# First attention of a two-layer block on one core: heads in pairs, scores computed twice

## The chip, the core and the metric

The kernel runs on one core of a Trainium2 chip. The metric is the time of one execution on the device, in microseconds. PE is the matrix engine, PEld its weight loads, DVE the vector engine, ACT the scalar engine, POOL GpSimd, and SP the engine that issues most DMAs. Each engine runs its own instruction stream in order; they meet at semaphores (`then_inc`, `wait_ge`).

## The reference

The input x is 4 x 512 rows of 256. Everything is computed in float32:

```
_L0_attn_ref:                     # 16 heads of 16, causal, B = 4, S = 512
q, k, v = heads(x @ Wq.T), heads(x @ Wk.T), heads(x @ Wv.T)
sim = where(causal, (q @ k.T) * 16 ** -0.5, -inf)
out = merge(softmax(sim) @ v) @ Wo.T

x = x + layernorm(_L0_attn_ref(layernorm(x), Wq, Wk, Wv, Wo))
x = x + layernorm(_L0_ffn_ref(layernorm(x), ...))
```

`_L0_ffn_ref` is a second causal attention (16 heads of 128), a shared gated layer and 16 routed experts of which each row takes four.

## The kernel before

Rows are in tiles of 128, four tiles to a batch. After the projections (phase 1, to the first `meet`) q and k lie transposed and split in a high and a low fp32r part, `q1_hl` (in the memory of `xT`) and `k1_hl`; v lies in `v1` (the memory of `hs`), all for 8 groups of 8 heads (128 rows are 8 heads of 16). A score in nearly full precision needs hi x hi + lo x hi + hi x lo. So a head's operands are stacked in 64 rows of `stk`: three copies of 16 rows, and one matmul sums the three products.

In the first attention 64 heads follow each other, a step (`step1`) each, written out except for a loop over two periods (`run_steps`). The engines work as a pipeline, with the values one step behind the scores:

- PE, every second head: `stack` selects the operands of a pair with a 0/1 matrix `sel` (L1462), into the banks 5 and 6; ACT copies them to `stk` (L769).
- PE: `scores`, four matmuls for the query tiles of 512, 384, 256 and 128 keys (L1545), banks 0 to 2.
- DVE: `mask_and_max` adds the causal mask in PSUM and gives the negated maximum of each query (L1092). ACT: the exponential into `p1`, with the sum (L816). DVE: reciprocal and multiplication (L1162, L1168).
- PE: `turn`, ten 128 x 128 transposes of the probabilities (L1555); DVE and ACT copy them to `pT1` (L1146, L825).
- PE: `values_of`, four fp32 matmuls against `v1_pad`, the head's 16 columns of v in 128 otherwise zero columns (L1567), so that 8 heads add up in bank 7 (`O1_BANK`). POOL fills `v1_pad` (`fill_v`, L455) up to six heads ahead. After 8 heads DVE copies bank 7 to `oT1`.

Between batches the finished batch is projected (`project_y`), normalised, added to x (`make_x1`) and normalised twice more for the second layer, spread over the steps of the next batch: PE and ACT for the copies, POOL for a chain of small operations on four numbers a row (`norm_y` and `norm_x1`, with `rsqrt` by three Newton steps, each operation waiting for the one before in `link`), ACT and DVE for the scaling (`scale_u`, `scale_xn`). What is left of the last batch runs beside the second attention. POOL also splits the weights of the second attention's first pair, before its first `fill_v` of the loop.

SP loads the inputs, issues one DMA that blanks 34 MB of `xs_rows` in HBM for the expert stage (L373), and then waits for the end of the first attention.

## Time and profile before

| | us |
|---|---|
| median of 3 runs (1417.71 to 1421.4) | 1419.59 |
| the profiled execution | 1434.26 |
| its span, first to last instruction | 1432.5 |
| PE busy in the span | 1306.9 (91%) |
| DVE busy | 1022.8 (71%) |
| ACT busy | 894.2 (62%) |
| POOL busy | 528.8 (37%) |

The granted clock of PE was 0.968 of full speed over the span. Busy time is the time in which at least one instruction of the engine was in work; matmuls overlap in the records, and an fp32 matmul has two records. In rows, a time in us comes first, then a duration; brackets at the end say how long the engine had been idle and who ended that.

### The profile page before, as it was taken

The numbers are of one execution on the slowest core, as the hardware profiler recorded it, in microseconds if no ns is written. First come the engines' busy times: TensorE is split into PE (matmuls) and PEld (weight loads), VectorE is DVE, ScalarE is ACT, GpSimd is POOL, SyncE is SP. The second block draws the span as 40 slices with busy tenths as digits, with TensorE's granted clock in tenths as the row PEclk, the third lists the DMA queues.
The fourth block names the chain that finished last, engine by engine and source line by source line (L and its number), as shares of the span: only waits on it lengthen the run. The fifth ranks groups of instructions, "written<-read, shape, count | busy, mean of one in ns | idle before, by whom it ended". The sixth has DMA issues, their size and how long they took to land.

```text
span 1432.5 us, 27089 instructions
## 1 busy us (share of the span) xinstructions
PE 1306.9 (91%) x7836; PEld 1125.4 (79%) x7836; DVE 1022.8 (71%) x3118; ACT 894.2 (62%) x2433; POOL 528.8 (37%) x868
## 2 busy tenths in 40 slices
PE   5999989989989989999999999999998878999940
PEld 4766766667669979999999899998997757999930
DVE  6588888978956757677877678667876655555536
ACT  3577766767757668776786767876676542444422
POOL 1300230412333344354364424734335251444434
PEclk9999999999999999999999999999999998999975
DMA  9993000000011331101122111211021333333353
GB/s 333 335 335 103 2 1 2 1 0 1 1 32 51 99 105 60 60 31 60 49 86 74 53 38 60 86 64 60 30 72 48 109 101 98 117 119 120 116 200 134
DMA packets 83615, 123.38 MB, mean 86 GB/s; under 512 B 7476, under 2 KB 68148, under 8 KB 83220
## 3 DMA queue, kind: packets, MB, share of 16 engines
q1 hardware_dynamic: 76612, 102.83, 22.5%
q0 software_dynamic: 6864, 18.88, 3.6%
q8 instruction: 65, 1.06, 0.3%
q14 instruction: 74, 0.61, 0.1%
HBM read 66.50 MB, written 55.18 MB: 85 GB/s over the span
## 4 chain that ended last, share of the span: by engine, by line
PE 71%; DVE 12%; issue 5%; ACT 4%; POOL 3%; DMA 2%; SPq 2%; another core or an unknown queue 1%; POOLq 0%; DVEq 0%; ACTq 0%
PE bank L1462 45%; PE bank L1567 8%; PE bank L1823 5%; PE bank L1641 4%; PE bank L1555 3%; DVE bank L1092 3%; PE bank L1545 3%; PE bank L1802 1%; PE bank L1833 1%; DVE hs L1313 1%; ACT p L928 1%; DMA yl<-ys_rows 1%; SPq L383 1%; DVE pT L1300 1%
## 5 line engine op out<-in xcount | busy, mean ns | idle before, releaser
L1092 DVE CUSTOM_DVE_ANT_0 bank<-bank,mask 128x512 f32<-128x512 f32 (+3 forms) x512 | 238.8, 518 | 36.3 <-PE bank L1545 18.3
L919 ACT ACTIVATE p<-bank,stat 128x512 f32<-128x512 f32 (+3 forms) x256 | 131.5, 526 | 133.3 <-DVE stat L1092 133.2
L1567 PE MATMUL bank<-pT,v_pad 128*128 128x128 f32 (+3 forms) x512 | 181.6, 457 | 17.3 <-DVE pT L1146 17.2
L1462 PE MATMUL bank<-xT,w_hl 128*128 128x512 f32 x768 | 190.2, 397 | 3.5 <-DVE hs L1313 3.0
L1462 PEld LDWEIGHTS bank<-xT,w_hl 128*128 128x128 f32 x768 | 145.4, 190 | 38.0 <-issue 3.5
L466 POOL CAST w_hl<-raw_qkv 128x512 fp32r<-128x512 f32 x96 | 58.9, 614 | 312.2 <-DMA raw_qkv<-in_qkvo 163.2
L816 ACT ACTIVATE p<-bank,stat 128x512 f32<-128x512 f32 (+3 forms) x256 | 133.0, 530 | 57.9 <-DVE stat L1092 57.9
L1462 PE MATMUL bank<-pT,v 128*128 128x128 f32 (+3 forms) x768 | 137.0, 327 | 0.0
L1462 PE MATMUL bank<-qk 128*128 128x512 f32 (+3 forms) x768 | 131.1, 320 | 3.0 <-DVE pT L1300 2.6
L928 ACT ACTIVATE p<-p,stat 128x512 f32<-128x512 f32 (+3 forms) x256 | 123.1, 552 | 15.2 <-DVE stat L1316 14.7
L1462 PEld LDWEIGHTS bank<-qk 128*128 128x128 f32 x768 | 120.6, 191 | 12.1 <-DVE v L1294 2.8
L468 POOL TENSOR_TENSOR w_hl<-raw_qkv,w_hl 128x512 fp32r<-128x512 f32 x96 | 124.0, 1292 | 7.8
L1567 PEld LDWEIGHTS bank<-pT,v_pad 128*128 128x128 f32 x512 | 86.1, 193 | 49.9 <-DVE pT L1146 24.8
L1338 DVE TENSOR_TENSOR o<-bank,o 128x512 fp32r<-128x512 f32 x64 | 44.2, 690 | 111.1 <-ACT o L935 91.3
L705 POOL DMA_INDIRECT ys_rows<-mid,goal x79 | 76.5, 968 | 126.5 <-DVE mid L1419 123.9
L1555 PEld LDWEIGHTS bank<-ident,p 128*128 128x128 f32 x640 | 81.3, 143 | 44.2 <-DVE p L1168 19.2
L1462 PEld LDWEIGHTS bank<-pT,v 128*128 128x128 f32 x768 | 109.7, 190 | 2.9
L1462 PE MATMUL bank<-wo_hl,o 128*128 128x256 f32 x768 | 106.9, 288 | 3.3 <-DVE o L1338 1.4
L1462 PEld LDWEIGHTS bank<-w_hl,xT 128*128 128x128 f32 x768 | 99.8, 189 | 12.2 <-issue 4.4
L1300 DVE TENSOR_TENSOR pT<-bank,pT 128x128 fp32r<-128x128 f32 (+3 forms) x256 | 107.5, 482 | 1.4 <-issue 1.0
L1462 PE MATMUL bank<-w_hl,xT 128*128 128x256 f32 x768 | 102.8, 283 | 4.5 <-POOL w_hl L468 2.6
L1555 PE MATMUL bank<-ident,p 128*128 128x128 f32 x640 | 104.1, 277 | 2.7 <-DVE p L1168 2.6
(243 smaller groups left out, 2886.5 us busy)
## 6 DMA issues: line engine op xcount, KB each, us to landing
xs_rows<-blank SPq DMA_DIRECT2D x1, 33410.0 KB, 115.1
raw_qkv<-in_qkvo SPq DMA_DIRECT2D x32, 768.0 KB
xrow<-xs_rows SPq DMA_DIRECT2D x79, 130.0 KB, 2.1
raw_o<-in_qkvo SPq DMA_DIRECT2D x32, 256.0 KB
yl<-ys_rows SPq DMA_DIRECT2D x16, 512.0 KB, 9.4
w_raw<-in_moe SPq DMA_DIRECT2D x12, 320.0 KB, 5.0
x_sb<-in_x SPq DMA_DIRECT2D x4, 512.0 KB, 6.6
out<-x_sb SPq DMA_DIRECT2D x4, 512.0 KB, 3.0
```

The costliest lines, as they stand in the source:

```text
L466: pool.tensor_copy(hi, raw).then_inc(b_half, 1)
L468: pool.tensor_tensor(lo, raw, f32(hi), ALU.subtract).then_inc(done, 1)
L705: pool.indirect_dma_start(ys_d, bass.IndirectOffsetOnAxis(goal[:, i % NY:i % NY + 1], 0), yt[:, i % NY, :], None).then_inc(y_sent[i % NY], 16)
L816: act.activation(p1[:, k % 2, POFF[qi]:POFF[qi + 1]], s1(t), ACT.Exp, scale=-1.0, bias=stat1[:, 0, k % 2, t:t + 1], accum_out=stat1[:, 1, ...
L919: act.activation(p2[:, n % 2, POFF[qi]:POFF[qi + 1]], s2(t), ACT.Exp, scale=-1.0, bias=stat2[:, 0, n % 2, t:t + 1], accum_out=stat2[:, 1, ...
L928: act.activation(pt, pt, ACT.Copy, scale=stat2[:, 2, n % 2, t:t + 1]).then_inc(b_norm, 1)
L1092: return dve.tensor_tensor_reduce(scores, scores, mask[:, TB - scores.shape[1]:], scale=-1.0, scalar=-2.0 * MASKED, op0=ALU.add, op1=ALU.m ...
L1300: dve.tensor_tensor(pT2[:, LO, QOFF[kj]:QOFF[kj + 1]], bank[t][:, 0:TB - P * kj], f32(pT2[:, HI, QOFF[kj]:QOFF[kj + 1]]), ALU.subtract).th ...
L1462: ins = pe.matmul(out, a, b, start=start and i == 0, stop=stop and i == len(pairs) - 1, **kw)
L1555: ins = pe.transpose(bank[PT1_BANK[t % 2]][:, P * (qi - kj):P * (qi - kj + 1)], p1[:, (k - 1) % 2, POFF[qi] + P * kj:POFF[qi] + P * (kj + 1)],
L1567: pe.matmul(bank[O1_BANK][:, P * kj:TB], v1_pad[:, kj, prev, :], pT1[:, QOFF[kj]:QOFF[kj + 1]], start=(prev == 0 and t == 0), stop=(prev = ...
L1823: ins = pe.matmul(bank[6 + i % 2][:, 0:D], ht[:, i % 2, P * h:P * (h + 1)], w2r[:, ds(expert[i], 1), h, :].rearrange("p a n -> p (a n)"), ...
```

## The change

The first attention goes over 32 pairs of heads, one `step1(s)` each, all written out. A pair's two heads (a = 0, 1) use rows 0-63 and 64-127 of `stk`.

- `stack`, `sel` and the copies by ACT go. SP fills one of four slots of `stk` per pair with 14 DMAs inside the on-chip memory (`load_stack`); four slots are filled ahead of the first `meet`. In 16 rows that were free stands one row of ones against the keys' side and one for the maximum against the queries' side, cleared first by two of the DMAs.
- Scores are computed twice. By query (`score`) they serve only for the maximum: DVE writes the negated maxima into columns 0 and 64 of `least`, PE transposes it, and ACT copies the two rows into `stk` (`a1_m`). By key (`score_t`) they come out with the maximum already subtracted; five exponentials of 128 x 512 go straight to `pT1` as the transposed probabilities. The transposes of the probabilities and their copies go.
- The causal mask is applied to the diagonal blocks after the exponential, by POOL (`clear_future`, four `affine_select` a pair).
- `v1_pad` has 32 columns a head: 16 of v, one of ones (which gives the sum) and zeros. `value` writes 32 rows of bank 6 for each head, so four heads fill it; the two heads alternate. Every second pair ACT copies it to `o1_sum`, PE transposes it, and DVE divides by the sum (`weigh`); every fourth pair PE transposes the result again, into `oT1`.
- The blanking of `xs_rows` is one DMA a pair (`prefill`).
- POOL takes the two roots of `norm_x1` at once (`roots(2)`); ACT scales all four tiles in `scale_u` and `scale_xn`. POOL splits the second attention's weights in steps 0 to 3.

The core of the diff (waits of single batches, projections and `weigh` are cut):

```diff
+        ITEMS = {4: (0, 1), 3: (3, 4), 2: (2, 2), 1: (3, 4)}
+        S1_PARTS, S1_REST = ((0, 4), (1, 4), (0, 2)), ((0, 3), (1, 3), (0, 1), (1, 1))
+        N1 = B * H1 // 2
+        O1_BANK, FREE_BANK = 6, 7
+        def item(a, n):
+            return ITEMS[n][a], 2 * P * a if n == 2 else 3 * P if n == 1 else 0
+        def s1(a, n):
+            first = 3 * P if n == 1 else 0
+            return bank[2 if n == 2 else a][:, first:first + P * n]
+        def st1(s, i):
+            return bank[3 + (5 * s + i) % 3]
+        def pt1(s, a, n):
+            i, first = item(a, n)
+            return pT1[:, s % 2, i, first:first + P * n]
...
-            sp.dma_start(sel_raw[:, :], stack_d).then_inc(sel_in, 16)
...
+            def load_stack(s):
+                slot, g, first = s % NSTK, s // (GH // 2), 2 * DH1 * (s % (GH // 2))
+                if s >= NSTK:
+                    sp.wait_ge(a1_st, 6 * (s - NSTK + 1))
+                for w, src, part, row in ((0, q1_hl, HI, 1), (0, q1_hl, LO, 2), (0, q1_hl, HI, 3),
+                                          (1, k1_hl, HI, 1), (1, k1_hl, HI, 2), (1, k1_hl, LO, 3)):
+                    for a in range(2):
+                        to = slice(64 * a + DH1 * row, 64 * a + DH1 * (row + 1))
+                        sp.dma_start(f32(stk[to, slot, w, :]),
+                                     f32(src[first + DH1 * a:first + DH1 * (a + 1), g, part, :])).then_inc(stk_in[slot], 16)
+                for a in range(2):
+                    sp.dma_start(f32(stk[64 * a:64 * a + 1, slot, 0, :]), f32(stk[64 * a + 1:64 * a + 2, slot, 0, :]))\
+                      .then_inc(stk_in[slot], 16)
+            def prefill(s):
+                xs = xs_d.rearrange("(n p) c -> p n c", p=P)
+                each = E * CAP // P // N1
+                some = slice(each * s, each * (s + 1) + (1 if s == N1 - 1 else 0))
+                sp.dma_start(xs[:, some, :], blank[:, :].unsqueeze(1).to_broadcast([P, some.stop - some.start, ROW]))\
+                  .then_inc(d_zero, 16)
+            sp.wait_ge(stk_zero, 3)
+            sp.wait_ge(ph1_lo, 4)
+            for s in range(NSTK):
+                load_stack(s)
+            meet(sp, 0)
             sp.wait_ge(d_blank, 2)
-            sp.dma_start(xs_d.rearrange("(n p) c -> p n c", p=P),
-                         blank[:, :].unsqueeze(1).to_broadcast([P, E * CAP // P + 1, ROW])).then_inc(d_zero, 16)
-            meet(sp, 0)
+            for s in range(N1):
+                if s >= NSTK:
+                    load_stack(s)
+                prefill(s)
...
+            pool.memset(f32(stk[:, :, :, :]), 0.0).then_inc(stk_zero, 1)
...
+            def fill_v(s):
+                g, first = s // (GH // 2), 2 * DH1 * (s % (GH // 2))
+                if s >= 2:
+                    pool.wait_ge(a1_pv, s - 1)
+                pool.tensor_copy(v1_pad[:, s % 2, :, :, 0:DH1],
+                                 v1[:, g, :, first:first + 2 * DH1].rearrange("p j (a n) -> p j a n", a=2))\
+                    .then_inc(a1_vpad, 1)
+            def clear_future(s):
+                own = pT1[:, s % 2, :, :]
+                diagonals = (own[:, 0:2, 0:P], own[:, 2, :].rearrange("p (a n) -> p a n", a=2)[:, :, 0:P],
+                             *(own[:, i, :].rearrange("p (c n) -> p c n", c=TPB)[:, ::TPB - 1, :] for i in (3, 4)))
+                for part, taken in zip(diagonals, (2, 3, 4, 5)):
+                    pool.wait_ge(a1_exp, 5 * s + taken)
+                    pool.affine_select(out=part, in_=part, compare_op=ALU.is_ge, fill=0.0, base=0,
+                                       pattern=[[0, 2], [1, P]], channel_multiplier=-1).then_inc(a1_sel, 1)
...
+            def step1(s):
+                fill_v(s)
+                clear_future(s)
+                b, k = s // (N1 // B) - 1, s % (N1 // B)
...
+                if b >= 0 and k == 2:
+                    norm_y(b)
+                if b >= 0 and k == 4:
+                    make_x1(b)
+                if b >= 0 and k == 5:
+                    norm_x1(b)
...
+            def step1(s):
+                b, k = s // (N1 // B) - 1, s % (N1 // B)
+                def exp(i):
+                    act.wait_ge(a1_st, 6 * s + (i + 1 if i < 2 else i + 2))
+                    if i == 0 and s >= 2:
+                        act.wait_ge(a1_pv, s - 1)
+                    act.activation(pT1[:, s % 2, i, :], st1(s, i)[:, :], ACT.Exp).then_inc(a1_exp, 1)
+                if s < N1:
+                    act.wait_ge(a1_mt, s + 1)
+                    for a in range(2):
+                        act.activation(stk[64 * a:64 * a + 1, s % NSTK, 0, :], free[64 * a:64 * a + 1, :], ACT.Copy)\
+                           .then_inc(a1_m, 1)
...
+                if s < N1:
+                    for i in range(3):
+                        exp(i)
+                if s >= 2 and s % 2 == 0:
+                    act.wait_ge(a1_pv, s)
+                    act.wait_ge(a1_ot, s // 2 - 1)
+                    act.activation(o1_sum[:, :], bank[O1_BANK][:, :], ACT.Copy).then_inc(a1_oe, 1)
...
+                if b >= 0 and k == 4:
+                    scale_u(b)
+                if b >= 0 and k == 7:
+                    scale_xn(b)
...
+                if s < N1:
+                    for i in range(3, 5):
+                        exp(i)
+                if b >= 1 and k in (0, 1):
+                    scale_hs(b - 1, k)
...
+                def row_max(a, *sizes):
+                    for n in sizes:
+                        ins = mask_and_max(s1(a, n), least[:, (s + 1) % 2, n - 1, 64 * a:64 * a + 1])
+                    ins.then_inc(a1_max, 1)
+                def weigh(i):
+                    dve.wait_ge(a1_ot, i + 1)
...
+                if s + 1 < N1:
+                    if s >= 1:
+                        dve.wait_ge(a1_mt, s)
+                    for i, (a, n) in enumerate(S1_PARTS):
+                        dve.wait_ge(a1_s, 6 * (s + 1) + i + 1)
+                        row_max(a, n)
+                if s >= 3 and s % 2 == 1:
+                    weigh((s - 3) // 2)
...
+                if s + 1 < N1:
+                    for i, (a, *sizes) in enumerate(((0, 3, 1), (1, 3, 1), (1, 2))):
+                        dve.wait_ge(a1_s, 6 * (s + 1) + i + 4)
+                        row_max(a, *sizes)
...
+                if b >= 0 and s < N1 and k == 5:
+                    x1_stats(b)
...
+                def score(r, a, n):
+                    rows, m, qi = slice(64 * a, 64 * a + 64), r % NSTK, n - 1
+                    return pe.matmul(s1(a, n), stk[rows, m, 0, P * qi:P * (qi + 1)], stk[rows, m, 1, 0:P * n],
+                                     start=True, stop=True)
+                def score_t(a, n):
+                    rows, m, kj = slice(64 * a, 64 * a + 64), s % NSTK, TPB - n
+                    i, first = item(a, n)
+                    return pe.matmul(st1(s, i)[:, first:first + P * n], stk[rows, m, 1, P * kj:P * (kj + 1)],
+                                     stk[rows, m, 0, P * kj:TB], start=True, stop=True)
+                def value(r, a, n):
+                    kj, j = TPB - n, 2 * (r % 2) + a
+                    return pe.matmul(bank[O1_BANK][2 * DH1 * j:2 * DH1 * (j + 1), P * kj:TB], v1_pad[:, r % 2, kj, a, :],
+                                     pt1(r, a, n), start=n == TPB, stop=n == 1, skip_group_check=True)
+                r = s + 1
+                if r < N1:
+                    pe.wait_ge(stk_in[r % NSTK], 16 * 14 * (r // NSTK + 1))
+                    for i, (a, n) in enumerate(S1_PARTS):
+                        if r >= 1:
+                            pe.wait_ge(a1_max, 6 * (r - 1) + i + 4)
+                        score(r, a, n).then_inc(a1_s, 1)
+                if 0 <= s < N1:
+                    if s >= 1:
+                        pe.wait_ge(a1_m, 2 * s)
...
+                    pe.wait_ge(a1_max, 6 * (s + 1))
+                    turn(lambda j: least[:, s % 2, j, :], a1_mt, free)
+                if 1 <= s <= N1:
+                    if s % 2 == 1 and s >= 3:
+                        pe.wait_ge(a1_oe, s // 2)
+                    pe.wait_ge(a1_vpad, s)
+                    pe.wait_ge(a1_sel, 4 * (s - 1) + 1)
+                    for a in range(2):
+                        value(s - 1, a, TPB)
+                if 0 <= s < N1:
+                    pe.wait_ge(a1_m, 2 * (s + 1))
+                if s >= 3 and s % 2 == 1:
+                    if s == N1 + 1:
+                        pe.wait_ge(m_lo, C * (B - 1))
+                    pe.wait_ge(a1_oe, (s - 1) // 2)
+                    turn(lambda j: o1_sum[:, P * j:P * (j + 1)], a1_ot, free)
...
+                if r < N1:
+                    for a, n in S1_REST:
+                        if n == 3:
+                            pe.wait_ge(a1_max, 6 * r + 1 + a)
+                        ins = score(r, a, n)
+                        if n == 1:
+                            ins.then_inc(a1_s, 1)
+                    pe.wait_ge(a1_max, 6 * r + 3)
+                    score(r, 1, 2).then_inc(a1_s, 1)
+                if 0 <= s < N1:
+                    for i, (a, n) in enumerate(S1_PARTS):
+                        if s >= 1:
+                            pe.wait_ge(a1_exp, 5 * (s - 1) + i + 3)
+                        score_t(a, n).then_inc(a1_st, 1)
+                if 1 <= s <= N1:
+                    pe.wait_ge(a1_sel, 4 * s)
+                    for n in range(TPB - 1, 0, -1):
+                        for a in range(2):
+                            ins = value(s - 1, a, n)
+                    ins.then_inc(a1_pv, 1)
...
+                if 0 <= s < N1:
+                    pe.wait_ge(a1_st, 6 * s + 3)
+                    score_t(1, 2).then_inc(a1_st, 1)
+                    for a, n in S1_REST:
+                        if n == 3:
+                            pe.wait_ge(a1_exp, 5 * s + 1 + a)
+                        ins = score_t(a, n)
+                        if n == 1:
+                            ins.then_inc(a1_st, 1)
...
```

## Rows read from the trace of the kernel before

**Rows 1.** Windows, first attention: length, busy us of PE, PEld, DVE, ACT, POOL; clock, DMA

```profile
56.20:405.60 349.40, 327.82 (x1608) 234.85 (x1608) 298.46 (x1138) 243.72 (x741) 79.05 (x274) 0.98 0.20 61
```

**Rows 2.** Timeline: first selection matmul, last batch's output products

```profile
56.16 0.50 PE L1462 MATMUL bank<-xT,sel 128*128 128x512 f32 x1 [0.78 <-ACTq L269]
...
405.65 3.72 PE L1462 MATMUL bank<-wo,oT 128*128 128x256 f32 x16 [0.84 <-DVEq L269]
```

**Rows 3.** Chain of waits over one pair: start, us, what

```profile
79.62 0.77 PE bank L1545 x4
80.39 0.42 PE bank L1567 x2
...
81.14 0.43 PE bank L1567 x2
81.57 0.44 PE bank L1555 x4
82.01 0.93 PE bank L1462 x4
82.94 1.50 PE bank L1567 x4
...
85.23 0.38 DVE bank L1092
...
89.46 0.77 PE bank L1545 x4
```

**Rows 4.** Timeline: weight loads of one head's scores

```profile
225.97 0.70 PEld L1545 LDWEIGHTS bank<-stk 64*128 64x128 f32 x4 [0.17 <-issue]
```

**Rows 5.** ACT, timeline and groups: copies and exponentials of 512

```profile
229.95 1.10 ACT L769 ACTIVATE stk<-bank 128x512 fp32r<-128x512 f32 x2
...
L816 ACT ACTIVATE p<-bank,stat 128x512 f32<-128x512 f32 x63 | 43.3, 688 | 57.7 <-DVE stat L1092 57.7
...
175.77 1.13 ACT L782 ACTIVATE mid<-mid,midst 128x256 f32<-128x256 f32 x2
```

**Rows 6.** Timeline: DVE, first maximum of a head, end of its third

```profile
226.66 0.70 DVE L1092 CUSTOM_DVE_ANT_0 bank<-bank,mask 128x512 f32<-128x512 f32 x1 [0.41 <-PE bank L1545]
...
228.18 0.14 DVE L1092 DVE_READ_ACCUMULATOR2_ANT stat<- 128x1 f32 x1
```

**Rows 7.** Timeline: POOL, a selection, a memset, a fill of v_pad

```profile
1.73 0.28 POOL L433 TENSOR_SCALAR_AFFINE_SELECT ident<-ident 128x128 f32<-128x128 f32 x1 [0.25 <-POOL xn_mid L431]
...
56.17 3.52 POOL L450 MEMSET v_pad<- 128x4096 f32 x1 [44.22 <-ACTq L269]
...
161.22 0.24 POOL L455 COPY v_pad<-hs 128x64 f32 x1 [6.09 <-PE bank L1567]
```

**Rows 8.** SP's issues by tile (ns min/median/max), the blanking's issue and landing

```profile
L404 SPq DMA_DIRECT2D w2r<-in_moe x52: 291/354/1303, 1132.0 to 1190.3; - x52
...
L414 SPq DMA_DIRECT2D xrow<-xs_rows x79: 337/338/386, 1191.7 to 1361.5; - x79
...
L383 SPq DMA_DIRECT2D w_raw<-in_moe x28: 328/640/2536, 493.0 to 1125.8; - x28
...
7.43 0.44 SPq L373 DMA_DIRECT2D xs_rows<-blank  x1
...
xs_rows<-blank SPq DMA_DIRECT2D x1, 33410.0 KB, 115.1
```

**Rows 9.** Timeline of phase 1: batch 0's keys split, the selection copied

```profile
24.53 1.91 ACT L751 ACTIVATE sel<-sel_raw 128x2048 fp32r<-128x2048 f32 x1
...
25.34 1.28 DVE L1082 SCALAR_TENSOR_TENSOR k_hl<-bank,k_hl 128x512 fp32r<-128x512 f32 x2
```

**Rows 10.** Timeline: first and last of the layernorm chain (23 operations), then x1

```profile
166.59 0.21 POOL L512 TENSOR_TENSOR midst<-mid 128x4 f32<-128x4 f32 x1 [5.13 <-DVE mid L1097]
...
174.66 0.35 POOL L528 TENSOR_SCALAR midst<-midst 128x4 f32<-128x4 f32 x1 [0.20 <-POOL midst L527]
177.28 2.35 POOL L535 TENSOR_TENSOR mid<-x_sb,mid 128x1024 f32<-128x1024 f32 x1 [2.27 <-ACT mid L782]
```

More of the change, by code:

```diff
@@ L29 @@
 ROOT_GUESS = 1597463007.0
-def run_steps(eng, step, total, period, first, ahead):
-    loops = (total - first - ahead) // period
-    for k in range(first):
-        step(0, k)
-    with eng.Fori(0, loops) as it:
-        for k in range(first, first + period):
-            step(it, k)
-    for k in range(first, total - loops * period):
-        step(loops, k)
 def sandwich_kernel(nc, x_d, qkv1_d, wo1_d, qkvo2_d, ln_w_d, gate_d, moe_d, stack_d, out_d):
@@ L579, in _ @@
+            for s in range(N1):
+                step1(s)
             meet(pool, 1)
-            norm_y(B - 1, 0)
+            norm_y(B - 1)
             steps = [0]
@@ L764, in _, with take_y @@
             meet(act, 0)
-            def take_stack(m_par, count):
-                for w in range(2):
-                    act.wait_ge(a1_sel, count + w + 1)
-                    act.activation(stk[:, m_par, w, :], bank[STK_BANK[w]][:, :], ACT.Copy).then_inc(a1_stk, 1)
-            def take_y(batch, extra, half, bank_):
-                act.wait_ge(m_y, batch * 2 + (extra * 2 + half + 1))
-                if half == 0 and (not isinstance(batch, int) or batch + extra):
-                    act.wait_ge(m_hs, batch * TPB + extra * TPB)
+            def take_y(b, half, bank_):
+                act.wait_ge(m_y, 2 * b + half + 1)
+                if half == 0 and b:
+                    act.wait_ge(m_hs, TPB * b)
@@ L856, in _, with scale_u, scale_xn @@
-            run_steps(act, step1, N1 + 1, PER1, PER1 + 2, 5)
+            def scale_u(b):
+                act.wait_ge(m_nrm, b + 1)
+                for j in range(TPB):
+                    act.activation(mid[:, j, :], mid[:, j, :], ACT.Identity, bias=midst[:, OFF, j:j + 1],
+                                   scale=midst[:, RSTD, j:j + 1]).then_inc(m_ua, 1)
+            def scale_xn(b):
+                act.wait_ge(m_rms, b + 1)
+                for j in range(TPB):
+                    act.activation(xn_mid[:, j, :], mid[:, j, :], ACT.Identity, bias=midst[:, OFF2, j:j + 1],
+                                   scale=midst[:, RSTD2, j:j + 1]).then_inc(m_xna, 1)
@@ L857, in _ @@
+            for s in range(N1 + 2):
+                step1(s)
             meet(act, 1)
             for half in range(2):
-                take_y(B - 1, 0, half, bank[LAST_Y_BANK[half]])
+                take_y(B - 1, half, bank[LAST_Y_BANK[half]])
             def squares(b):
@@ L1187, in _ @@
+            for s in range(-1, N1 + 2):
+                step1(s)
             meet(dve, 1)
             for half in range(2):
-                y_stats(B - 1, 0, half)
+                y_stats(B - 1, half)
             offset = sm[:, 7, :]
@@ L1498, in _ @@
                     ins.then_inc(ph1_mm, 1)
-            pe.wait_ge(sel_ok, 1)
             meet(pe, 0)
-            def stack(g, pair):
-                for w, src in enumerate((q1_hl, k1_hl)):
-                    product(bank[STK_BANK[w]][:, :],
-                            [(sel[:, P * (4 * pair + 2 * w + a):P * (4 * pair + 2 * w + a + 1)], src[:, g, a, :])
-                             for a in (HI, LO)]).then_inc(a1_sel, 1)
             def project_y(half, bank_):
@@ L1516, in project_y @@
                 ins.then_inc(m_y, 1)
-            def turn_mid(batch, extra, banks):
-                for half_done in (m_xna, m_xnd):
-                    pe.wait_ge(half_done, batch * 2 + (extra * 2 + 2))
-                for c in banks:
-                    for j in range(TPB):
-                        ins = pe.transpose(bank[banks[c]][:, P * j:P * (j + 1)], xn_mid[:, j, P * c:P * (c + 1)],
-                                           ident[:, :])
-                    ins.then_inc(m_tp, 1)
-            pe.wait_ge(wo1_in, 16)
@@ L1603, in _, with turn, turn_mid @@
-            run_steps(pe, step1, N1 + 1, PER1, PER1 + 2, 5)
+            def turn(src, done, bank_):
+                for j in range(TPB):
+                    ins = pe.transpose(bank_[:, P * j:P * (j + 1)], src(j), ident[:, :])
+                ins.then_inc(done, 1)
+            def turn_mid(b, c, bank_):
+                pe.wait_ge(m_xna, TPB * (b + 1))
+                turn(lambda j: xn_mid[:, j, P * c:P * (c + 1)], m_tp, bank_)
+            pe.wait_ge(wo1_in, 16)
+            free = bank[FREE_BANK]
@@ L1604, in _ @@
+            for s in range(-1, N1 + 2):
+                step1(s)
             meet(pe, 1)
```

506 lines of the change are left out of this document (160 added, 346 removed).

## The prediction

> **What bounds the kernel now.** I read the windows first, to see how long the first attention lasts and how full its engines are. It runs from the first selection matmul at 56.16 us to the first output product at 405.65 us [rows 2], 349.4 us, with PE busy for 327.8 us of it, DVE for 298.5, ACT for 243.7, POOL for 79.1 [rows 1]. PE is what this stage is short of, and DVE is close behind.
>
> The chain of waits then shows one pair of heads [rows 3]. Score groups of two heads start at 79.62 and 89.46: 9.84 us a pair. Each head costs PE 0.77 us for four score matmuls and 0.42 + 0.43 + 1.50 = 2.35 us for its eight value records. Ten transposes at 0.11 (0.44 for four) are 1.10, and the selection products are 0.93 for the pair. That is 2 x (0.77 + 2.35 + 1.10) + 0.93 = 9.37 us of 9.84. The small rest is DVE's mask-and-maximum, on which the chain sits from 85.23 because the odd head has no selection products to cover it. So only less PE work per pair can shorten the stage much, and 32 pairs of 9.84 are 315 us; the other 35 us are the output projections, the layernorms between batches and the ends.
>
> **The change, PE first.** Removed per pair: 20 transposes of the probabilities (2.20 us) and the selection products (0.93). Added: a second set of scores, by key, so 16 score matmuls instead of 8, and transposes of maxima (4), of sums (4 every second pair) and of results (4 every fourth), on average 7 x 0.11 = 0.77 us. The values keep their columns, but each head now uses 32 columns of the array, and the scores alternate between rows 0-63 and 64-127.
>
> No row shows two tiles of the array at work together, so both prices are bounded. If nothing overlaps, scores cost 4 x 0.77 = 3.08 us and values 2 x 2.35 = 4.70. If the two heads of a pair run side by side, 1.54 and 2.35. The nearest row is the score matmul [rows 3]: it already uses one half of the rows and leaves the other idle, and the new order puts the other head, with its own rows, columns and PSUM bank, straight behind. I take the lower end. Each change of tile shape costs up to the 0.17 us of issue ahead of the score loads [rows 4]; there are about six in a step, 1.0 us, where nothing would be the lower bound.
>
> The Trainium skill, page "TensorE: Matmul & The Clock Gate", section on packing small matmuls, reports 2.38 times for three column tiles and 3.07 for four row tiles. By it the low prices hold. Page "TensorEngine Tiling (Array Packing)", Key Properties, says that changing the tiling mode drains the engine, which speaks against six changes in a step; by it the 1.0 us stays in the sum, and the 0.17 us row agrees with it.
>
> New is a wait on PE's path: the transposed maxima go through ACT, which copies two one-row strips of 512 before the dependent scores. The two-copy row takes 1.10 us [rows 5], plus some 0.25 until ACT starts; the first values (0.86 of the 2.35) cover most, leaving 0.5 us. Behind the waiting PE stand all later scores, and DVE and ACT wait for those. Another 0.2 us I give to the two exponentials that free score banks. Step: 1.54 + 2.35 + 0.77 + 1.0 + 0.5 + 0.2 = 6.4 us.
>
> **The other engines in a step.** DVE: eight maxima. From the start of a head's first to the end of its third are 1.52 us [rows 6], and the last, of 128, is put at 0.20, so 2 x 1.72 = 3.4 us. The normalising multiplications and half the copies go; weighing adds about 0.4. Under 4.5 us. ACT: five exponentials of 512 at 0.5 to 0.69 are 2.5 to 3.4 us, 1.1 for strips, 0.45 for two copies on average: below 5.0. POOL: four selections over 256 columns, between 0.28 (128 columns) and twice that, some 1.8 us, and a copy of 0.25 [rows 7]. All hide under 6.4.
>
> SP is the new suspect. A pair needs 14 small DMAs and one prefill: 15 issues where the loop had none. Small issues took 291 to 1303 ns, median 354, others a steady 338 [rows 8]; with 0.04 between them 14 are 5.5 us and the 0.44 of the large one makes 5.9. That is half a microsecond under the step, and four slots give three pairs of lead. The bounds are 4.7 (all at 291 ns plus gaps) and 9.6 (all at the 640 ns of w_raw). The bytes are no limit: the prefill, 115.1 us for all, is 3.6 us a pair in 32 parts, and the stack's 0.4 MB about 1.2 at the same rate, 4.8 in all. The first four loads are 56 issues, 22 us. They begin when batch 0's keys are split, at 26.6 us [rows 9], and end near 49, ahead of 56.16; the lower bound is 45 us and at 640 ns each they would end near 64, 8 us late. The selection copy taken from ACT (1.91 us) lay beside PE's value products, so I count nothing; if it were exposed it would give back 1.9 at most. Clearing the stacks on POOL at the start (4096 columns, as the 3.52 us memset) puts POOL's weight split 2 to 3 us later, hidden since PE first needs it at 16.2; without that cover it costs 3.
>
> The Trainium skill, page "DMA: Bandwidth & Descriptors", Rules for kernel authors, wants small transfers coalesced, as those under 64 KB mostly pay overhead; these have 32 KB. The rows agree that the issue does not shrink with the bytes.
>
> **Between batches.** Three times, PE does output products (3.72 us in the last batch [rows 2]) and eight transposes (0.88): 4.6 us, as now. What changes is POOL. Its chain of 23 small layernorm operations takes from 166.59 to 175.0, 8.4 us [rows 10]; the change cuts the second one from two roots in series to two at once, also about 8.4. But POOL now must clear the diagonals before the next values, where before it only filled v_pad, six heads ahead. From the end of its pair the queue has 8.4 + 0.25 + 0.45 us ahead of the first clearing, and PE wants it 1.15 us into the second next step, 7.5 us later: a stall of about 2. The same behind the 3.6 us of x1 (2.35 and its copy) about 1, and behind the second chain, which starts later, about 4.5. ACT takes all of scale_u and scale_xn: four activations where 1.13 us for two stood, one more us each for two queues, and DVE waits for x1. Together 12.4 us a batch. Bounds: nothing, if slack eats them, and three whole chains, 20 us.
>
> **The sum.** 32 x 6.4 = 205; 3 x (4.6 + 12.4) = 51; filling (two memsets and the ones on POOL before DVE may start, first maxima of eight tiles) 6 and draining 5. That is 267 us for 349.4: a gain of 82. The second attention and the experts keep their work. The profiled execution took 1434.3 us around its 1432.5 span, so it becomes 1352; the median of the runs stood 14.7 lower, at 1419.6, so 1337.
>
> **The rivals.**
> - Only scores or only values overlap. Step 6.4 + 2.35 - 0.5 = 8.2 or 6.4 + 1.54 = 7.9; POOL's stalls halve as the step grows: 32 x 8.0 + 14 + 20 + 11 = 301, so 1371. For it: values in fp32 come as two records each, so their order is less regular.
> - Nothing overlaps: 3.08 + 4.70 + 0.77 + 0.6 = 9.2 a step, 294 + 14 + 9 + 11 = 328, so 1398. For it: no row shows an overlap. The kernel still wins a little since 9.84 had three stages in series.
> - SP's queue sets the pace. At 640 ns an issue a pair takes 9.6 us: 32 x 9.6 + 10 + 8 late = 325, so 1395.
> - The other side: SP's issues cost over 0.73 us. The stage is slower by 4 us when 32 pairs take over (353 - 10) / 32 = 10.7 us, that is (10.7 - 0.44) / 14 = 0.73 us each. At 0.8 a pair is 11.6, the start is 15 late, the stage 396: 1466. The maximum of 1303 ns speaks for it, the median of 354 against.
> - POOL's and ACT's bursts vanish in slack: 205 + 14 + 11 = 230, so 1300.
>
> **How the numbers follow.** Chances: forecast 0.58 (its own range 1310 to 1365 from a step of 6.0 to 6.9 and bursts of 6 to 16), one overlap 0.17, none 0.11, SP at about 640 ns 0.04, SP dearer than 0.73 0.05, bursts vanish 0.05. Leaving out the dear SP, part of the no-overlap case and half of the last gives 1300 to 1396. Within 0.3% (4 us, what a measurement here can tell from no change) is only the tail of the no-overlap case: 0.03. Faster 0.92, slower 0.05.
>
> **What would show it.** The score groups by query should start 6.4 us apart away from batch changes. Of two matmuls of a pair the second should start right behind the first and both end together; if starts are 0.21 us apart at 512 columns, nothing overlaps. SP's issues should lie near 0.35 us with pauses before a1_st; without pauses SP is the bound. PE should wait for ACT's strips about 0.5 us a pair, and for POOL's selections only in three steps of each batch. The prediction is wrong above all if tiles don't overlap, or if an SBUF-to-SBUF issue is dearer than any row here.

## The result, and the profile after

| | before | after |
|---|---|---|
| median | 1419.88 us (1417.71 to 1421.4) | 1430.53 us (1428.47 to 1430.88) |
| ratio after/before | | 1.0073, 95% interval 1.0056 to 1.0091 |
| profiled span | 1432.5 us | 1428.6 us |
| loop of the first attention starts | 56.16 | 67.33 |
| last batch's output products start | 405.65 | 413.25 |

The kernel became 10.7 us slower; 1337 us was forecast, with 1300 to 1396 as the range. The profile of before lay 14.4 us above its median and that of after at it, so the two spans are no measure of the change. The marks inside the stage are: it ends 7.6 us later, of which 11.2 us are a later start and -3.6 us a shorter loop. The other 3 us of the medians' difference lie outside the stage or between one execution and the next; the two profiles can't tell. All ratios compare executions in the chip's faster state; one execution of experiment 6, 2226.81 us at a granted clock of 0.81, was in the slower one and is left out.

First two windows of after, with the columns of [rows 1]:

```profile
56.00:140.00 84.00, 55.33 (x291) 28.56 (x291) 34.22 (x141) 32.26 (x60) 22.17 (x47) 0.74 0.49 146
140.00:240.00 100.00, 68.74 (x397) 34.95 (x395) 42.05 (x171) 44.06 (x83) 29.94 (x96) 0.83 0.45 133
```

PE's work is gone as forecast: 69 of 100 us are busy where it was 94 [rows 1], part of that at a lower clock. But no engine is full now, so something else sets the step. PE's timeline over one pair names it (the bracket is the idle time before, and what ended it):

```profile
211.59 0.85 PE L1483 MATMUL bank<-stk 64*128 64x512 f32 x3 [2.80 <-DMA stk<-stk]
...
216.10 1.49 PE L1496 MATMUL bank<-pT,v_pad 128*32 128x384 f32 x12
217.52 0.62 PE L1490 MATMUL bank<-stk 64*128 64x256 f32 x5
222.28 1.00 PE L1483 MATMUL bank<-stk 64*128 64x512 f32 x3 [4.14 <-DMA stk<-stk]
```

PE finishes a step in 6.5 us (211.59 to 218.1) and then stands idle for 4.14 us until the last DMA into the next stack, the clearing one, has landed. The waits add this up: 26 times, some 91 us.

```profile
PE bank L1483 <- DMA stk<-stk: 90.9, 26, 6.0
```

That DMA is late because SP issues it late. SP's operations on the stacks by tile (ns min/median/max, then first and last start), and SP's timeline from the first blankings on:

```profile
L359 SPq DMA_DIRECT2D stk<-xT x192: 507/589/1427, 29.8 to 381.2; - x192
L362 SPq DMA_DIRECT2D stk<-stk x64: 581/589/597, 38.3 to 386.7; - x64
...
67.41 5.54 SPq L370 DMA_DIRECT2D xs_rows<-blank  x4
79.77 4.04 SPq L359 DMA_DIRECT2D stk<-xT  x6
...
87.64 1.22 SPq L362 DMA_DIRECT2D stk<-stk  x2
88.90 0.58 SPq L370 DMA_DIRECT2D xs_rows<-blank  x1
89.53 4.98 SPq L359 DMA_DIRECT2D stk<-xT  x6
94.55 5.07 SPq L359 DMA_DIRECT2D stk<-k_hl  x6
```

The groups follow each other without a pause, to the end at 387.9 us: 28 pairs in 308 us, 11.0 us a pair. An issue takes 0.589 us and 0.04 to the next, so 15 are 9.45 us; the other 1.55 us are single long issues. The second and third issue behind every blanking take 1.38 and 1.00 to 1.17 us, together some 1.25 us over the common price. The other 0.3 us a pair come from one more long issue, of 0.85 to 1.74 us, in about every third pair. In the chain of waits:

```profile
89.53 0.59 SPq L359
90.11 0.04 issue
90.16 1.38 SPq L359
...
91.58 1.03 SPq L359
...
92.65 0.59 SPq L359
...
94.55 1.74 SPq L359
```

So SP's queue of issues is the bound, at 11.0 / 15 = 0.73 us an issue with all that lies between.

### The profile page after: what moved, and what is told of

The parts are those of the page before. It is cut to its first block, busy times and chain, and to the rows that moved or that the text cites. A ratio compares the mean times of both kernels' runs of the same rounds, so it can differ in the third digit from the quotient of the medians.

```text
span 1428.6 us, 24397 instructions
## 1 busy us (share of the span) xinstructions
PE 1217.0 (85%) x7548; PEld 1010.1 (71%) x7548; DVE 867.8 (61%) x2550; ACT 809.9 (57%) x1992; POOL 563.6 (39%) x901
## 3 DMA queue, kind: packets, MB, share of 16 engines
q8 instruction: 65, 1.06, 0.3%
## 4 chain that ended last, share of the span: by engine, by line
PE 55%; SPq 24%; DVE 8%; issue 4%; ACT 3%; POOL 3%; DMA 2%; POOLq 0%; ACTq 0%; DVEq 0%
PE bank L1417 41%; SPq L359 19%; PE bank L1804 5%; PE bank L1622 4%; SPq L362 3%; DVE bank L1077 2%; PE bank L1783 1%; PE bank L1814 1%; ACT p L913 1%; POOL xs_rows L646 1%; SPq L370 1%; DVE hs L1272 1%; DMA yl<-ys_rows 1%; SPq L390 1%; DMA raw_qkv<-in_qkvo 1%
## 5 line engine op out<-in xcount | busy, mean ns | idle before, releaser
L1077 DVE CUSTOM_DVE_ANT_0 bank<-bank,mask 128x512 f32<-128x512 f32 (+3 forms) x512 | 235.9, 522 | 174.5 <-PE bank L1483 147.9
L904 ACT ACTIVATE p<-bank,stat 128x512 f32<-128x512 f32 (+3 forms) x256 | 131.5, 526 | 132.6 <-DVE stat L1077 132.6
L1483 PE MATMUL bank<-stk 64*128 64x256 f32 (+3 forms) x256 | 54.5, 453 | 104.8 <-DMA stk<-stk 90.9
L485 POOL TENSOR_SCALAR_AFFINE_SELECT pT<-pT 128x256 f32<-128x256 f32 x128 | 51.6, 406 | 220.4 <-ACT pT L801 217.7
L801 ACT ACTIVATE pT<-bank 128x512 f32<-128x512 f32 x160 | 87.9, 599 | 84.9 <-PE bank L1490 84.4
L1483 PEld LDWEIGHTS bank<-stk 64*128 64x128 f32 x256 | 33.2, 240 | 133.5 <-DMA stk<-stk 96.2
L1496 PE MATMUL bank<-pT,v_pad 128*32 128x256 f32 (+3 forms) x512 | 100.5, 518 | 1.1 <-POOL pT L485 0.7
```

Of the source, the lines that this page charges most:

```text
L801: act.activation(pT1[:, s % 2, i, :], st1(s, i)[:, :], ACT.Exp).then_inc(a1_exp, 1)
L904: act.activation(p2[:, n % 2, POFF[qi]:POFF[qi + 1]], s2(t), ACT.Exp, scale=-1.0, bias=stat2[:, 0, n % 2, t:t + 1], accum_out=stat2[:, 1, ...
L1077: return dve.tensor_tensor_reduce(scores, scores, mask[:, TB - scores.shape[1]:], scale=-1.0, scalar=-2.0 * MASKED, op0=ALU.add, op1=ALU.m ...
L1483: return pe.matmul(s1(a, n), stk[rows, m, 0, P * qi:P * (qi + 1)], stk[rows, m, 1, 0:P * n], start=True, stop=True)
L1496: return pe.matmul(bank[O1_BANK][2 * DH1 * j:2 * DH1 * (j + 1), P * kj:TB], v1_pad[:, r % 2, kj, a, :], pt1(r, a, n), start=n == TPB, stop ...
```

## The experiments

Times of a chip differ from the next one's by over 1%, so kernels are compared by their ratio to before on the same chip: before had 1435.85 us beside the first four, 1437.33 beside the next four, 1423.48 beside the last three. "Stage" is the time from the first score matmul to the last batch's output products in the profile, 345.9 us in after.

**1. The whole blanking issued once by ACT, ahead of the loop.** SP has 14 issues a pair.

```
-                prefill(s)                      # SP, each step
+            act.dma_start(xs_d..., blank...)    # ACT, once, before the loop
```

> The blanking of xs_rows goes back to one DMA, issued by ACT ahead of the loop, so SP has 14 issues a pair and not 15, and no large transfer in its own queue. Theory 1, SP's issue time alone sets the pace (0.63 us for each at the common 0.59 + 0.04): 0.63 x 28 = 18 us less, 1412. Theory 2, the large transfers stretch SP's issues (11.0 us a pair against 15 x 0.63 = 9.45, an excess of 1.55): 28 x (0.63 + 1.55) = 61 us less, 1370. Rival, the engines' own step is already as long as SP's: no change, 1430.

Measured: 1450.42 us, ratio 1.0096 (1.0064 to 1.0129). Fewer issues, and no gain. SP's timeline while the big transfer is under way, and that transfer's row (KB, us to landing):

```profile
150.35 8.96 SPq L359 DMA_DIRECT2D stk<-k_hl  x6
159.35 2.94 SPq L362 DMA_DIRECT2D stk<-stk  x2
...
176.82 3.75 SPq L359 DMA_DIRECT2D stk<-xT  x6
...
xs_rows<-blank ACTq DMA_DIRECT2D x1, 33410.0 KB, 109.9
```

Each issue takes some 1.47 us there, not 0.59, and the first four pairs of the loop take 19 to 22 us each. Once the transfer has landed, a pair takes 8.85 us (176.82 to 185.67), which is 14 issues at 0.63, and 9.1 on average. An issue's time is no constant of SP: it grows while much blanking is in flight. The cost of the blanking was not removed, it was paid in one stretch.

**2. The two clearing DMAs left out.** The scores by query do read the row that they clear, beside the row of ones. Without the clearing it holds the shift of four pairs before, which moves all scores of a query by one amount; the softmax stays the same.

```
-                for a in range(2):
-                    sp.dma_start(f32(stk[64*a:64*a+1, slot, 0, :]), f32(stk[64*a+1:64*a+2, slot, 0, :]))
```

> The two DMAs that clear the maximum's row of a slot are left out; the row keeps the shift of four pairs before, which moves a query's scores all by one amount and leaves the softmax the same. 13 issues a pair instead of 15. Theories 1 and 2: 2 x 0.63 x 32 = 40 us less, 1390 (the first four loads end 5 us sooner too). Rival, engines as long as SP: 1430.

Measured: 1406.81 us, ratio 0.9792 (0.9765 to 0.9819). Two issues of 2 KB each, out of 15, turn the loss into a gain. SP's timeline:

```profile
160.85 4.99 SPq L359 DMA_DIRECT2D stk<-xT  x6
...
170.30 2.02 SPq L359 DMA_DIRECT2D stk<-xT  x2
```

This pair is 9.45 us; on average over the loop a pair is 9.76, 1.3 less than in after, which is the two issues at 0.63. The excess stays. The first stacks are ready 5 us sooner too (the loop starts at 62.19).

**3. No loads after the first four pairs.** Later pairs work on the stacks of old heads, so the results of those heads are not the reference's; the engines' work is the same.

```
             for s in range(N1):
-                if s >= NSTK:
-                    load_stack(s)
                 prefill(s)
```

> Leaves out the stack loads of all pairs but the first four, so later pairs work on old heads. SP is out of the way inside the loop. Theory 1 and 2: what is left is the engines' step as forecast, 6.4 us and 17 us around each batch change, stage 267 us, started 11 us late: 1348. If the array's tiles do not overlap, 1398 + 11 = 1409. If the engines are as slow as SP: 1430.

Measured: 1372.47 us, ratio 0.9569 (0.9542 to 0.9596). The stage is 270.4 us (67.11 to 337.55), where 267 was forecast for it. ACT's strips, one group a step:

```profile
111.68 1.20 ACT L804 ACTIVATE stk<-bank 1x512 fp32r<-1x512 f32 x2
117.54 1.18 ACT L804 ACTIVATE stk<-bank 1x512 fp32r<-1x512 f32 x2
```

Away from batch changes the engines need 5.9 us a step (forecast 6.4).

**4. The twelve loads of a pair move 128 of the 512 columns.** The rest of a stack keeps old data.

```
-    sp.dma_start(f32(stk[to, slot, w, :]), ...)
+    sp.dma_start(f32(stk[to, slot, w, 0:P]), ...)
```

> The twelve loads of a pair move 128 of the 512 columns, the rest of the stack keeps old values; the count of DMAs stays. Theory 1, the count decides: 1430. Rival, the bytes in the queue push back on SP: the excess of 1.55 us a pair goes, 28 x 1.55 = 43 us, 1387, and more if the common 0.59 us is made of bytes too.

Measured: 1445.06 us, ratio 1.0069 (1.0049 to 1.0089), the same as after.

```profile
L359 SPq DMA_DIRECT2D stk<-xT x192: 507/589/1686, 29.8 to 378.5; - x192
```

With a quarter of the bytes the issue keeps its 0.589 us. The count decides, not the stacks' bytes. The long issues stay too (1.38 and 0.96 to 1.06 us behind each blanking), so they don't come from the stacks' bytes either; whether from the blanking, experiment 9 tests.

**5. Do two column tiles work at once?** On top of experiment 3, twelve of sixteen value records head after head.

```
-                    for n in range(TPB - 1, 0, -1):
-                        for a in range(2):
+                    for a in range(2):
+                        for n in range(TPB - 1, 0, -1):
```

> The run without loads after the first four pairs, with the value products of three of the four key tiles issued head after head (3 + 3) instead of alternately. Work is the same. Theory 1 (two column tiles work side by side, which only alternating order uses): the twelve records that took 1.49 us take about 2.56, so a step is 1.1 us longer where PE sets the pace; a step has about 0.5 us of slack there, so 0.6 to 1.1 us x 32, 1392 to 1408 us where the run without this edit gave 1372.5 (ratio 0.970 to 0.981). Rival (the records overlap only in the trace's modelled ends): no difference, ratio 0.957.

Measured: ratio 0.9642 (0.9609 to 0.9675), 0.0073 or some 10 us above experiment 3; the stage is 282.6 us for 270.4. The same group in PE's timelines, first of experiment 3 with its neighbours, then of this one:

```profile
244.98 0.51 PE L1481 MATMUL bank<-stk 64*128 64x384 f32 x4 [0.31 <-ACT stk L804]
...
245.82 1.49 PE L1494 MATMUL bank<-pT,v_pad 128*32 128x384 f32 x12
247.24 0.56 PE L1488 MATMUL bank<-stk 64*128 64x256 f32 x4
...
248.08 0.66 PE L1465 MATMUL bank<-ident,least 128*128 128x128 f32 x4
```

```profile
163.43 2.16 PE L1494 MATMUL bank<-pT,v_pad 128*32 128x384 f32 x12
```

The same twelve records take 2.16 us instead of 1.49, and an undisturbed step 6.5 us instead of 5.9. The clock is not the reason: four transposes take 0.66 us in both places. That is 0.65 us in undisturbed steps, and less in those that wait for POOL or ACT anyway, so the whole costs less than my 20 us. The overlap is real and not one of modelled ends; the serial work is less than the 2.56 us that I had put for it.

For the scores no run changed the order. The rows of experiment 3 speak for an overlap: eight score products lie between 244.98 and 245.82 and the other eight between 247.24 and 248.08, so a step's sixteen take 1.68 us, where before eight took 1.54 [rows 3].

**6. ACT issues six of the twelve loads.**

```
+                if s + NSTK < N1:
+                    for to, frm in stack_moves(s + NSTK)[:6]:
+                        act.dma_start(to, frm).then_inc(stk_in[s % NSTK], 16)
```

> Everything as in the changed kernel, but ACT issues six of the twelve loads of the pair four ahead, at the end of its own step. Theory 1 (one queue's issue time sets the pace): SP has 9 issues, about 5.7 + 1.5 us; ACT's 4.9 us of work a step plus 6 x 0.6 is 8.5 us, so steps come to 8.5 to 9 us where they were 11.0, ratio 0.95 to 0.975. Rival (the issue time is a limit of the DMA system that both queues share): the issues of both queues stretch to 1.2 us, a pair stays near 11 us and ACT is held up as well: ratio 1.00 to 1.03.

Measured: ratio 1.0155 (1.0104 to 1.0206). Theory 1 missed. The ratio lies in the rival's range, but not for its reason: SP's issues are not stretched to 1.2 us, their median stays 0.589. SP was relieved, and the stage got longer (369 us). SP now pauses (of the 12.0 us from 211.24 to 223.24 it issues for 5.5), and ACT's timeline and the sum of PE's waits say why:

```profile
211.24 3.69 SPq L368 DMA_DIRECT2D stk<-k_hl  x6
...
223.24 3.69 SPq L368 DMA_DIRECT2D stk<-k_hl  x6
...
201.18 3.55 ACTq L847 DMA_DIRECT2D stk<-xT  x4
204.77 1.20 ACT L814 ACTIVATE stk<-bank 1x512 fp32r<-1x512 f32 x2 [3.72 <-issue]
...
PEld bank L1478 <- ACT stk L814: 59.1, 14, 5.8
```

On ACT an issue costs about the same (median 0.612 us, up to 1.985), and ACT's strips of the next step stand behind it in program order. PE waits for the strips, and the other engines for PE. I had added ACT's busy times; the step is a chain through ACT, and up to 3.7 us of issues now stand on it (57.4 us in 24 steps). The Trainium skill, page "DMA: Bandwidth & Descriptors", Rules for kernel authors, says that spreading DMAs over engines only saves issue time of a sequencer. The trace agrees: it saved SP's and spent ACT's. In this kernel ACT's was the dearer.

**7. Two loads a pair, by way of HBM.** Queries and keys go to HBM once per group of eight heads, in the order of the stacks, and a head's 48 rows come back as one DMA. The clearing is left out as well.

```
+                for w, src, part, row in (... six parts ...)[some]:       # 2 in 3 steps of 4
+                    sp.dma_start(hl_d[g, :, row, :, w, :], f32(src[:, g, part, :]))
...
-                for w, src, part, row in (...):                           # 12 loads of 32 KB
+                for a in range(2):                                        # 2 loads of 192 KB
+                    sp.dma_start(f32(stk[64*a+DH1:64*(a+1), slot, :, :]),
+                                 hl_d[g, first // DH1 + a].rearrange("r d w c -> (r d) w c"))
```

> The twelve loads of a pair become two: the split queries and keys go to HBM once per group of eight heads, in the order in which the stacks hold them (six stores of 256 KB a group, two in each of three steps out of four), and a stack is loaded by one DMA of 48 partitions for each head; the two clearing DMAs are left out. SP then issues 4.5 DMAs a step where it issued 15, and 6 + 8 before the loop where it issued 56. Theory 1 (the number of SP's issues sets the pace): the stage runs at the pace of the run without loads (1372.5 us on that chip, ratio 0.957) and its loop starts at about 59 instead of 67 us, so a ratio of 0.951 (0.945 to 0.962) to the kernel before. Rival (SP is slow because of what is in flight, not because of the count): 4.5 issues beside more traffic stretch to 2 us or more each, 9 us a step, and the ratio stays at 0.97 or above. Second rival: stores and loads that go through HBM collide with the blanking, some 6 us of all 16 DMA engines a step against about 5; then loads come late and PE waits on them, ratio 0.96 to 0.98.

Measured: 1378.84 us, ratio 0.9584 (0.9542 to 0.9627), within theory 1's bounds. The stage is 288.6 us. The loop starts where phase 1 lets it, as it did in before:

```profile
58.97 0.61 PE L1491 MATMUL bank<-stk 64*128 64x512 f32 x3 [0.78 <-ACTq L257]
```

The rivals had a small part in it: beside the blanking SP's issues grow to 2 us and over, and one of the first steps took 13.4 us, with the longest of only two waits for a stack. PE's timeline there, and SP's later:

```profile
90.70 1.01 PE L1491 MATMUL bank<-stk 64*128 64x512 f32 x3 [7.23 <-DMA stk<-hl_rows]
```

```profile
114.95 4.14 SPq L366 DMA_DIRECT2D stk<-hl_rows  x2
```

Fewer issues is not all of it: a load of this kind takes SP 0.426 us (median, least 0.302) where a move from SBUF to SBUF took 0.589. The two were not separated.

**8. POOL's clearing moved behind its split of the weights** (on top of 7).

```
-            pool.memset(f32(stk[:, :, :, :]), 0.0)...     # first thing on POOL
             for i, cols in enumerate(...): ... ph1_wl
+            pool.memset(f32(stk[:, :, :, :]), 0.0)...
```

> As the run through HBM, and POOL clears the stacks (3.51 + 3.65 us) after the splitting of the weights instead of at the start. DVE's two one-column operations at 6.66 and 8.49 us took 1.60 and 1.62 us in the changed kernel, beside POOL's clearing of single rows, and 0.15 without it. Theory: this clearing makes the first phase 3 us late, so this kernel is 3 us faster than the one before it in this list (ratio lower by 0.002). Rival: the clearing only moves beside other DVE work (the normalised rows and the low halves of 12 to 20 us) and costs there as much: no difference.

Measured: ratio 0.9584 (0.9541 to 0.9628), no difference; the rival was right. DVE's normalisation starts 3 us sooner and takes 5 us more, beside POOL's split and clearing. DVE's timeline of after (the last line is a later normalisation with POOL idle), and then of this kernel:

```profile
6.66 1.60 DVE L1032 TENSOR_SCALAR sm<-sm 128x4 f32<-128x4 f32 x1
...
11.40 4.39 DVE L1047 TENSOR_SCALAR xn<-x_sb,sm 128x256 f32<-128x256 f32 x4
...
25.89 1.38 DVE L1047 TENSOR_SCALAR xn<-x_sb,sm 128x256 f32<-128x256 f32 x4
```

```profile
8.37 9.23 DVE L1055 TENSOR_SCALAR xn<-x_sb,sm 128x256 f32<-128x256 f32 x4
```

**9. Two blankings a step in the first half of the loop, none in the second** (on top of after).

```
-                prefill(s)
+                if s < N1 // 2:
+                    prefill(2 * s)
+                    prefill(2 * s + 1)
```

> The changed kernel with the blanking issued two at a time in the first sixteen steps and none in the last sixteen; the same 15 issues a pair on average. Theory (the excess of 1.55 us a pair over 15 x 0.63 comes from the issues that stand behind a blanking): a pair takes 14 x 0.63 + 2 x 0.62 + 3.1 = 13.2 us while there are two and 14 x 0.63 = 8.8 us after the last one, when the engines' bursts between batches begin to set steps instead, so the time as a whole is lower by up to 10 us or the same, ratio 0.998 to 1.008. Rival (the excess belongs to the stack loads themselves or to SP's wait on the slots): pairs in the second half stay near 10.4 us without a blanking.

Measured: ratio 1.0154 (1.0125 to 1.0184). In the chain of waits two blankings have four long issues behind them (one had two, above):

```profile
100.11 0.58 SPq L370
...
100.74 0.58 SPq L370
...
101.37 1.45 SPq L359
...
102.86 1.35 SPq L359
...
104.25 1.65 SPq L359
...
105.94 1.52 SPq L359
```

And in SP's timeline after the last blanking:

```profile
289.75 4.86 SPq L359 DMA_DIRECT2D stk<-xT  x6
...
299.92 3.75 SPq L359 DMA_DIRECT2D stk<-xT  x6
...
308.76 3.75 SPq L359 DMA_DIRECT2D stk<-xT  x6
```

A pair takes 13.7 us with two blankings (from 101.37 to 115.08; the others 13.2 to 14.3) and 8.84 without one, as the theory has it, so the blanking is the cause of the long issues behind it. My total was wrong for two reasons. The four blankings at the loop's start became eight, whose issues take 19.3 us from 67.71, so the loads of the loop began at 87.1 and not at 79.8. And without blanking only two of three pairs take some 8.84 us: the long issue of about every third pair is there too (4.86 us for six, where six take 3.75). So this one comes neither from a blanking just ahead nor, by experiment 4, from the stacks' bytes; its cause stays open. SP issued to the end of the loads with two pauses, of 0.34 us each, so the engines' bursts did not set the second half.

**10. Blanking out of the way** (on top of 7): six of 32 in phase 1, none in the first four steps.

```
+            for s in range(6):
+                prefill(s)                   # before the first stores
...
-                prefill(s)
+                if 4 <= s < N1 - 2:
+                    prefill(s + 2)
```

> The kernel with two loads a pair through HBM, and its blanking moved: six of 32 before the first stores (beside the first phase, which uses 0.42 of the DMA engines), none in the first four steps, then one a step. Theory: in the run through HBM one step at the start took 13.4 us where its neighbours took 6 to 7.5, since SP's stores and the first loads of the loop stood behind blanking; without it that step takes 6.5 and the kernel is 5 to 8 us faster, ratio 0.953 where that run had 0.958. Rival: six blankings ahead of the first stores make these and the first eight loads 15 us or more later (6 MB at about 250 GB/s are 25 us), the loop starts after 59 us, and the gain is lost or turns into a loss, ratio 0.958 to 0.965.

Measured: 1355.03 us, ratio 0.9521 (0.9492 to 0.9551). The 13.4 us step is 5.8 us now, and PE waits for no stack any more; strips of the first steps:

```profile
78.87 1.19 ACT L817 ACTIVATE stk<-bank 1x512 fp32r<-1x512 f32 x2
84.70 1.19 ACT L817 ACTIVATE stk<-bank 1x512 fp32r<-1x512 f32 x2
```

The stage is 274.2 us (58.88 to 333.05), 14.4 less than in experiment 7; by the ratios the gain is 0.0063 or 9 us for the 5 to 8 expected, and their intervals overlap a little. This kernel computes all that the reference asks and is the fastest that does, 68 us under before on its chip.

**11. One iteration instead of three in POOL's roots** (on top of 10; layernorms less exact).

```
-                for _ in range(3):
+                for _ in range(1):
```

> As the run above, with one iteration of three in POOL's two chains of reciprocal roots between batches (the layernorms are less exact). Each chain has 8 of its small operations fewer, 0.28 us each, 2.2 us. Theory (POOL's chain stands ahead of the selections that PE's values wait for, and makes the long steps of 10 to 11 us): each of six chains in the stage gives back about 2.2 us, 13 us in all, ratio lower by 0.009 than the run above. Rival (the bursts come from ACT's four activations of 0.5 us and PE's output products): nothing, or under 3 us.

Measured: 1339.22 us, ratio 0.9411 (0.9385 to 0.9437), 0.0110 or 15.7 us below experiment 10, for 13 expected. The stage is 263.0 us, 11.2 less. POOL's chains are a part of the long steps; what is left of these (7.8 to 11.5 us for one in two) was not taken apart.

## Why the prediction was wrong, by its steps

- **The failed step is SP's price.** I put 14 small issues at 0.354 + 0.04 us from rows of HBM loads [rows 8]. From SBUF to SBUF they took 0.589 + 0.04, min 0.507; no row of before shows such an issue. The median of w_raw in the same group, 640 ns, was the nearer row, and I kept it as a mere bound. I counted 5.9 us a pair; 15 at 0.63 are 9.45. That price is nearly the one of the rival "SP's queue sets the pace" (640 ns, 9.6 us a pair, chance 0.04). Its bounds had a slip: 9.6 leaves out the gaps of 0.04 that the forecast counts, with them it is 10.2 us a pair and 1414 us, outside my range; and the lower bound, all at 291 ns, is 5.0 us and not 4.7.
- **The second half of it is a cost that I had nowhere:** 1.55 us a pair of long issues, where I had counted for the blanking only its own 0.44 and its bytes. Experiments 1 and 9 show that some 1.25 of it come from the blanking, 4 excludes the stacks' bytes; 0.3 come from a long issue in every third pair, whose cause is open. Together 11.0 us a pair.
- **The rival "SP's issues cost over 0.73 us" came true** in its sum: in its own counting 11.0 us a pair are (11.0 - 0.44) / 14 = 0.75 us each, where 10.7 a pair breaks even. Not as a price: a common issue was 0.63, and the rest were the long ones. I gave it 0.05. It should have had the largest chance after the forecast: SP's 5.9 us a pair stood half a microsecond under the engines' 6.4 us, on a median from another kind of transfer.
- **The first stacks.** Forecast: 56 issues from 26.6, 22 us, ready at 49. Measured: from 29.76, since phase 1 ran 3 us late, to 66.86, 37.1 us. The start at 67.33 costs 11.2 us.
- **Clearing on POOL was not hidden.** I looked only at POOL's own queue. Its clearing of single rows stood beside two DVE operations that took 1.60 us instead of 0.16, and all of phase 1 followed. I had priced a lack of cover at 3 us, the size that came, but for the weight split in POOL's queue and not for DVE.
- **PE's step was right.** 6.4 forecast, 5.8 to 6.0 measured when SP doesn't hold it (experiments 3 and 10). The scores take 1.68 us for 1.54, the values some 2.4 for 2.35, the wait for ACT's strips 0.6 to 1.0 for 0.5. With 0.77 for transposes that is some 5.6, so 0.3 is left where I had put 1.2 for changes of tile shape and for score banks. The values overlap (experiment 5); that the scores do was read from rows alone. The Trainium skill, page "TensorE: Matmul & The Clock Gate", section on packing small matmuls, has column tiles work side by side; the trace agrees in kind, with 1.45 times for two, 2.16 to 1.49 us.
- **The bursts were mis-sized:** 4.6 + 12.4 us a batch. The stage of 274.2 us in experiment 10 less 32 x 5.9 and my 11 for filling and draining leaves 74, so 25 us a batch. POOL's chain is a named part of it (experiment 11: 3.7 us a batch for two thirds of the iterations).
- **The stage as a whole, without SP: 267 forecast, 270.4 and 274.2 measured.** Two errors, in the step (-16 us) and in the bursts (+23), nearly cancelled; the agreement is luck.
- Of the signs I named, "without pauses SP is the bound" is what the trace shows; starts 6.4 us apart are not, with 10 to 12 us instead.
- **PE's clock was left out.** All prices came from a stage with a granted clock of 0.98 [rows 1]. In after it is 0.74 to 0.83 and in experiment 10 0.80 to 0.93. Undisturbed steps run near the upper level of 2.4 GHz (0.97 from 100 to 150 us in experiment 10, the twelve values in 1.49 us), but in nine of experiment 10's 32 steps they take 1.70 to 2.78 us, for example behind a wait for POOL:

```profile
287.03 1.92 PE L1507 MATMUL bank<-pT,v_pad 128*32 128x512 f32 x4 [2.20 <-POOL pT L496]
...
290.35 2.77 PE L1507 MATMUL bank<-pT,v_pad 128*32 128x384 f32 x12
```

So slower PE work may be a part of the 25 us a batch; how large a part was not measured.

## What to carry to other kernels

A queue that only issues is an engine with a step time: count its issues, price each from a row of the same kind of transfer, and if there is none, let the dearest plausible row decide the chance. When the margin to the next bound is smaller than the doubt in one price, the chance is not 0.05. Cut the number of DMAs before anything else, with a layout in HBM if need be; moving them to an engine on the critical chain can cost more than it saves, as in experiment 6.

## What the runs showed of the hardware

- A DMA from SBUF to SBUF took SP 0.589 us to issue and 0.04 to the next, with 2, 8 or 32 KB alike; on ACT the median was 0.612 (0.515 to 1.985). A load of 192 KB from HBM took SP 0.426 (median, least 0.302), a blanking of 1040 KB 0.583.
- Behind each transfer of 1040 KB the second and third issue took 1.38 and 1.00 to 1.17 us; behind two of them in a row four issues took 0.95 to 2.15, mostly 1.3 to 1.5; while 33 MB were under way every issue took some 1.47 us. One further issue of 0.85 to 1.74 us came in about every third pair, with blanking or without.
- Two value products on different 32-column tiles, in turn, took 1.49 us where one tile after the other took 2.16, and undisturbed steps were 0.65 us shorter for it.
- POOL's clearing of single rows (6.44 to 10.1 us) stood beside DVE's 128x4 operation of 1.60 us, 0.16 without it, while DVE's operation on two 128x4 inputs at 6.58 us took 0.16 beside it. Four normalisations took 9.23 us beside POOL's split (3.6 us) and clearing (7 us), 4.39 beside the split alone and 1.38 with POOL idle.
